# Centring of the second channel norm: 128 tokens in one matmul, or 64 tokens on each half of the array

## The chip, the core and the metric

One core of a Trainium2 chip. The metric is the device time of one execution in microseconds (us). The engines work in parallel, each through its own list of instructions, and meet by semaphores: TensorE (PE, with its weight loads PEld), VectorE (DVE), ScalarE (ACT), GpSimd (POOL) and SyncE (SP), which issues DMAs. TensorE reads SBUF and writes PSUM, whose 8 banks of 512 floats in each of 128 partitions are the tensor PS here.

## What is computed

An image x of 8 x 32 x 64 x 64 (batch, channels, height, width) in float32 goes through two blocks. Cut to what matters:

```python
x = x + L0_conv(ln_c(x))      # spectral convolution, by DFT matmuls
t = to_tokens(x)              # a token: the 32 channels of a pixel
t = t + L0_ffn(ln_t(t))       # soft routing, 16 experts
x = from_tokens(t, x)
x = x + L1_conv(ln_c(x))      # four sweeps of a 9-tap convolution, row by row
t = to_tokens(x)
t = t + L1_ffn(ln_t(t))
```

ln_c takes the mean over the 32 channels of a pixel, and divides by the root of the variance. The change is in the second ln_c, ahead of the four sweeps.

## The kernel before

**Layout.** The 128 partitions of an image hold 4 batch entries x 32 channels; a row of 8192 floats has two batch halves of 4096 pixels. RA, RB, RC, RD (RC and RD are the halves of RCD) and RE are the large SBUF regions. Work goes in 8 groups of 1024 columns, each with one slot of two PSUM banks, ln_slot(g) = banks 2(g % 4) and 2(g % 4) + 1.

**A channel norm, group by group** (norm_tokens on each engine). centre_group(ln, g) on TensorE: eight matmuls; the weights (the stationary operand) are 128 columns of the image, that is 128 pixels, and the moving operand is the 128 x 128 matrix centre (in dft_sb), which subtracts the mean over each 32 channels. The result has a pixel per partition and 128 columns (batch, channel). A float32 matmul leaves two records on PE and two on PEld. Then ACT squares the slot into RE (line 780), DVE sums over 32 channels (line 912), ACT takes the root (line 762), and DVE the reciprocal (line 919) and the product (line 928, "norm g"). follower(g) on TensorE waits for that. In the second norm it is turn_rows: eight transposes (line 725) of the normed group back into the slot, which ACT copies to RD with drain_follower (line 769).

**The second norm.** Pixels of a group are taken 4 columns apart (src = RC[:, first + n % Q:first + BANK:Q], Q = 4), since the sweeps want them sorted by column modulo 4. It starts inside the first expert layer: 16 scatter matmuls of 512 columns (line 714) give the layer's output, DVE adds each to RC (line 940), and behind the sixth and the tenth (FED) TensorE does centring groups 0 and 1.

**What sets the order.** Each engine's order is written out by hand. TensorE: scatter matmuls with groups 0 and 1 between; follower 0; groups 2 and 3; then follower g and group g + 3 in turn; followers 5 to 7. Group g from 4 on needs follower g - 4 copied out of its slot; groups 2 and later need all 16 adds. DVE: six adds, sum 0, four adds, norm 0, sum 1, six adds, norm 1, sums 2 and 3, norm 2, then sum g + 1 ahead of norm g. ACT: Square g behind the copy of follower g - 3, then root g - 1. The convolution (TensorE line 745, DVE line 1141) starts when all copies are done. It and the pooling (line 664) use the halves of the array: two matmuls with 64 weight columns each, whose outputs go to partitions 0 to 63 and 64 to 127. So does the spectral mixing (line 533).

Of the kernel before, what the change touches and what calls it, by code (L numbers as in the profile page):

```python
# [21 lines left out]
MO = P // 2  # L22
# [18 lines left out]
def build_kernel(nc, x_in, dft, wspec, conv_w, conv_b, gate_w, gate_b, w1, w2, b2, own, out):  # L41
# [5 lines left out]
    with ExitStack() as ctx:  # L47
        def sb(name, shape, dt=F32):
            return ctx.enter_context(nc.sbuf_tensor(name, shape, dt))
# [5 lines left out]
        RA, RB, RCD = sb("RA", [P, NF]), sb("RB", [P, NF]), sb("RCD", [P, 2 * NF])  # L55
# [6 lines left out]
        centre, ident, fwd_w, fwd_h, inv_h, inv_w = (dft_sb[:, i, :] for i in range(6))  # L62
# [64 lines left out]
        def blk(region, n):  # L127

            return region[:, n * P:(n + 1) * P]

        def banks(b0, nb):
            return PS[:, b0:b0 + nb, :].rearrange("p k c -> p (k c)")
# [103 lines left out]
        def ln_slot(g):  # L236

            return banks(2 * (g % 4), 2)
# [195 lines left out]
        def _(pe):  # L434
# [9 lines left out]
            def centre_group(ln, g):  # L444

                if ln == 0:
                    pe.wait_ge(s_x[g], 16)
                else:
                    pe.wait_ge(s_ad, 2 * g + 2 if g < 2 else 16)
                if g >= 4:  # L450
                    pe.wait_ge(s_fd, 8 * ln + g - 3)
                for n in range(8):
                    if ln == 0:
                        src = blk(RA, 8 * g + n)
                    else:
                        first = 1024 * g + BANK * (n // Q)
                        src = RC[:, first + n % Q:first + BANK:Q]
                    m = pe.matmul(blk(ln_slot(g), n), src, centre, start=True, stop=True)  # L458
                m.then_inc(s_cen, 1)

            def norm_tokens(ln, follow):

                def follower(g):
                    pe.wait_ge(s_nrm, 8 * ln + g + 1)
                    follow(g).then_inc(s_ff, 1)

                if ln == 1:
                    follower(0)
                for g in range(2 * ln, 4):
                    centre_group(ln, g)  # L470
                for g in range(ln, 8):
                    follower(g)
                    if 1 <= g < 5:
                        centre_group(ln, g + 3)
# [20 lines left out]
            for l in range(2):  # L495
                m = pe.matmul(PS[:, 6 + l, 0:BL * NE], centre, gate_sb[:, l, :], start=True, stop=True)
# [50 lines left out]
            for c in range(NCH):  # L547
# [5 lines left out]
                for w, full, read in ((1, s_t1, s_tmp), (0, s_t0, s_comb)):  # L553
                    if c >= 2:
                        pe.wait_ge(read, c - 1)
                    for x in range(X8):
                        m = pe.transpose(blk(banks(4 * (c % 2) + 2 * w, 2), x), Z[:, c, x, w], ident)  # L557
# [60 lines left out]
            def experts(l):  # L618
# [87 lines left out]
                for k in range(16):  # L706
                    if k >= 4:
                        pe.wait_ge(s_ad, 16 * l + k - 3)
                    if l == 0:
                        bh, ch = divmod(k, 8)  # L710
                    else:
                        ch, bh = divmod(k, 2)
                    rhs = CW[l][:, ch * BANK:(ch + 1) * BANK]
                    pe.matmul(PS[:, 4 + k % 4, :], espread[:, BL * bh:BL * bh + BL, :].rearrange("p b o -> p (b o)"), rhs,  # L714
                              start=True, stop=True).then_inc(s_sc, 1)
                    if l == 0 and k in FED:
                        centre_group(1, FED.index(k))
# [15 lines left out]
            for bank in range(2 * len(CHAINS)):  # L733
                m = pe.matmul(PS[:, bank, 0:P], warm[:, :], warm[:, :], start=True, stop=True)
# [485 lines left out]
```

## Time and profile before

| | |
|---|---|
| time, median of 3 | 612.09 us (611.95, 612.09, 614.93) |
| profiled execution, span | 614.5 us (of the three times only 614.93 is as long as that) |
| TensorE busy, weight loads | 565.0 us (92%), 511.2 us (83%) |
| DVE, ACT, POOL busy | 351.7, 319.6, 115.1 us |
| mean granted TensorE clock | 0.967 of full speed |
| second channel norm | from about 240 to 292 us of the span |

The span runs from the first to the last instruction. "Busy" of TensorE counts a record from its start to its modelled end, so that overlapping records of a pipeline fill the time. The chain of waits is followed back from the last instruction, at each step to what released it. A granted clock of 1.00 is 2.4 GHz, of 0.50 is 1.2 GHz.

### The profile page before, as it was taken

The page shows a single profiled execution, that of the slowest core. Times are in us where ns is not written, and L with a number is a line of the kernel's source. Part 1 is how long each engine was busy: PE and PEld are TensorE (multiplying, and loading weights), DVE is VectorE, ACT ScalarE, POOL GpSimd, SP SyncE. Part 2 cuts the span into 40 slices and gives each one's busy share as a digit, 9 for nine tenths or more (in the row PEclk, how much of TensorE's full clock was granted, in tenths as well). Part 3 has the DMA queues.
Part 4 walks back from the last instruction along what each step waited for, and adds up shares of the span by engine and source line. Part 5 has one row for each costly group of instructions (what it writes and reads, how often), then busy time and mean ns, then how long its engine had stood idle before and what let it go on. Part 6 is the DMA issues. An engine that isn't in the chain of part 4 may idle for free.

```text
span 614.5 us, 22679 instructions
## 1 busy us (share of the span) xinstructions
PE 565.0 (92%) x9860; PEld 511.2 (83%) x9860; DVE 351.7 (57%) x813; ACT 319.6 (52%) x842; POOL 115.1 (19%) x240
## 2 busy tenths in 40 slices
PE   8978878999999899997999999969999999984997
PEld 8978877999998897797899988868888888984973
DVE  2657989557435943755455455435555455568736
ACT  4766979452348610254444444424445777568610
POOL 4000000000016000000233333383332034371000
PEclk9999999899999798998899999989999999998989
DMA  9830764060000000000000003340000144500007
GB/s 352 330 137 2 276 234 181 2 246 29 1 2 1 2 3 19 0 1 0 3 5 3 5 3 89 90 105 4 4 3 5 25 76 83 102 1 1 2 3 273
DMA packets 50250, 41.53 MB, mean 68 GB/s; under 512 B 44998, under 2 KB 45126, under 8 KB 48934
## 3 DMA queue, kind: packets, MB, share of 16 engines
q1 hardware_dynamic: 49304, 38.51, 19.4%
q8 instruction: 79, 1.29, 0.9%
q0 software_dynamic: 704, 1.18, 0.9%
q10 hardware_dynamic: 144, 0.39, 0.2%
q14 instruction: 19, 0.16, 0.1%
HBM read 27.49 MB, written 4.19 MB: 52 GB/s over the span
## 4 chain that ended last, share of the span: by engine, by line
PE 76%; DVE 12%; ACT 5%; POOL 4%; issue 2%; DMA 1%; SPq 0%; POOLq 0%; ACTq 0%
PE PS L745 38%; PE PS L458 6%; PE PS L714 5%; DVE RB L986 4%; PE PS L479 3%; PE PS L533 3%; PE PS L664 3%; PE PS L608 2%; PE PS L557 2%; PE PS L564 2%; POOL RCD L400 2%; POOL RE L397 2%; PE PS L578 2%; PE PS L638 2%; DVE sums L1025 1%
## 5 line engine op out<-in xcount | busy, mean ns | idle before, releaser
L745 PE MATMUL PS<-RE,conv_sb 128*64 128x64 f32 x6048 | 230.9, 229 | 5.1 <-DVE RE L1129 4.7
L745 PEld LDWEIGHTS PS<-RE,conv_sb 128*64 128x64 f32 x6048 | 205.3, 139 | 30.8 <-DVE RE L1129 5.4
L879 ACT COPY PS<-convb_sb 128x64 f32<-128x64 f32 x504 | 108.2, 215 | 113.3 <-DVE RE L1141 89.2
L1141 DVE SCALAR_TENSOR_TENSOR RE<-PS,RCD 128x64 f32<-128x64 f32 x252 | 56.6, 225 | 58.2 <-PE PS L745 50.1
L409 POOL COPY RCD<-RE 128x128 f32<-128x128 f32 x126 | 37.0, 294 | 166.6 <-DVE RE L1141 166.4
L1141 DVE SCALAR_TENSOR_TENSOR RE<-PS,RE 128x64 f32<-128x64 f32 x126 | 32.5, 258 | 27.9 <-PE PS L745 19.9
L808 ACT COPY RB<-PS 32x256 f32<-32x256 f32 x64 | 42.4, 662 | 7.5 <-PE PS L517 6.8
L986 DVE COPY RB<-PS 32x256 f32<-32x256 f32 x64 | 42.2, 659 | 6.0 <-PE PS L517 5.2
L1141 DVE SCALAR_TENSOR_TENSOR RE<-PS,RB 128x64 f32<-128x64 f32 x126 | 28.3, 225 | 28.1 <-PE PS L745 19.9
L479 PE MATMUL PS<-warm 128*128 128x128 bf16 x468 | 37.8, 253 | 7.1 <-ACT RCD L848 4.5
L533 PE MATMUL PS<-RE,RB 128*64 128x64 f32 x1024 | 33.6, 228 | 9.8 <-issue 4.1
L533 PEld LDWEIGHTS PS<-RE,RB 128*64 128x64 f32 x1024 | 32.5, 143 | 11.2 <-issue 6.2
L479 PEld LDWEIGHTS PS<-warm 128*128 128x128 bf16 x468 | 35.0, 116 | 8.1 <-ACT RCD L848 4.7
L912 DVE TENSOR_REDUCE sums<-RE 128x32 f32<-128x1024 f32 x16 | 19.4, 1218 | 34.1 <-ACT RE L780 34.1
L397 POOL TENSOR_TENSOR RE<-RA 128x1024 f32<-128x1024 f32 x3 | 5.7, 1892 | 173.7 <-ACT RA L841 173.7
L780 ACT ACTIVATE RE<-PS 128x1024 f32<-128x1024 f32 x16 | 16.2, 1021 | 33.1 <-PE PS L458 33.0
L1025 DVE TENSOR_REDUCE sums<-RE 128x32 f32<-128x1024 f32 x16 | 19.2, 1201 | 24.2 <-POOL RE L397 18.7
L458 PEld LDWEIGHTS PS<-dft_sb,RCD 128*128 128x128 f32 x128 | 30.5, 328 | 0.9 <-issue 0.5
L458 PE MATMUL PS<-dft_sb,RCD 128*128 128x128 f32 x128 | 30.8, 396 | 0.0
L769 ACT COPY RCD<-PS 128x256 f32<-128x256 f32 (+1 forms) x40 | 24.7, 692 | 11.0 <-PE PS L725 5.8
L827 ACT COPY RB<-PS 128x512 f32<-128x512 f32 (+1 forms) x24 | 16.2, 736 | 26.2 <-PE PS L564 26.2
L714 PE MATMUL PS<-RCD,espread 128*128 128x512 f32 x64 | 29.7, 618 | 0.0
(120 smaller groups left out, 780.1 us busy)
## 6 DMA issues: line engine op xcount, KB each, us to landing
RE<-wspec SPq DMA_DIRECT2D x8, 2048.0 KB, 8.8
RA<-x_in SPq DMA_DIRECT2D x8, 512.0 KB, 7.5
RCD<-x_in SPq DMA_DIRECT2D x1, 4096.0 KB, 13.3
out<-RA SPq DMA_DIRECT2D x8, 512.0 KB, 2.7
RCD<-RB SPq DMA_DIRECT2D x58, 64.0 KB, 2.5
RE<-RCD SPq DMA_DIRECT2D x32, 80.0 KB, 2.6
conv_sb<-conv_w SPq DMA_DIRECT2D x1, 768.0 KB, 20.0
w_sb<-w SPq DMA_DIRECT2D x2, 264.0 KB
```

What stands on the lines that cost most here:

```text
L409: pool.tensor_copy(o, i).then_inc(s_arc, 1)
L458: m = pe.matmul(blk(ln_slot(g), n), src, centre, start=True, stop=True)
L479: pe.matmul(PS[:, bank, 0:P], warm[:, :], warm[:, :], start=True, stop=True)
L533: m = pe.matmul(o[:, x % 2, y], XB[:, c % 2, x, 2 * y + a].rearrange("p r q b -> p (r q b)"), WR[:, c % 3, a, x, y, :], start=True, stop=True)
L714: pe.matmul(PS[:, 4 + k % 4, :], espread[:, BL * bh:BL * bh + BL, :].rearrange("p b o -> p (b o)"), rhs, start=True, stop=True).then_inc(s ...
L745: m = pe.matmul(conv_bank(s, u, c)[o:o + OC], conv_sb[:, s, d, o:o + OC], prev, start=False, stop=(d == 2), skip_group_check=True)
L769: m = act.copy(o, i)
L808: m = act.copy(o, i)
L879: act.copy(banks_of, convb_sb[:, s:s + 1].unsqueeze(2).to_broadcast([P, c1 - c0, n])).then_inc(s_seed, 1)
L986: m = dve.tensor_copy(o, i)
L1025: dve.tensor_reduce(sums[:, 32 * g:32 * g + 32], square[:, g % 2, 0:1024].rearrange("p (a c) -> p a c", c=C), AX_X, ALU.add).then_inc(s_su ...
L1141: dve.scalar_tensor_tensor(out=state[:, state_slot(s, u), b0:b1, 1:1 + HO], in0=conv_bank(s, u, c), scalar=0.0, in1=row_at(SRC[s], s, q, u ...
```

## The change

In the second norm each centring matmul becomes two. The one takes the first 64 of the 128 pixels as weights and writes partitions 0 to 63 of the same 128 PSUM columns, the other the last 64 and partitions 64 to 127; the moving operand is the whole matrix centre both times. The first norm keeps its matmul, now written in its own branch.

```diff
                 for n in range(8):
                     if ln == 0:
-                        src = blk(RA, 8 * g + n)
+                        m = pe.matmul(blk(ln_slot(g), n), blk(RA, 8 * g + n), centre, start=True, stop=True)
                     else:
                         first = 1024 * g + BANK * (n // Q)
                         src = RC[:, first + n % Q:first + BANK:Q]
-                    m = pe.matmul(blk(ln_slot(g), n), src, centre, start=True, stop=True)
+                        for a in range(2):
+                            toks = slice(MO * a, MO * (a + 1))
+                            m = pe.matmul(blk(ln_slot(g), n)[toks], src[:, toks], centre, start=True, stop=True)
                 m.then_inc(s_cen, 1)
```

MO is 64, Q is 4, BANK is 512. All lines behind it move down by two: 458 is 460 in the second norm, 714 is 716, 725 is 727.

TensorE, from the scatter matmuls to centring groups 2 and 3, before (form of the output; an x for equal instructions in a row):

```order
L714 MATMUL PS<-RCD,espread 128x512 x6
L458 MATMUL PS<-dft_sb,RCD 128x128 x8
L714 MATMUL PS<-RCD,espread 128x512 x4
L458 MATMUL PS<-dft_sb,RCD 128x128 x8
L714 MATMUL PS<-RCD,espread 128x512 x6
L725 MATMUL PS<-dft_sb,RA 128x128 x8
L458 MATMUL PS<-dft_sb,RCD 128x128 x16
L725 MATMUL PS<-dft_sb,RA 128x128 x8
```

and after:

```order
L716 MATMUL PS<-RCD,espread 128x512 x6
L460 MATMUL PS<-dft_sb,RCD 64x128 x16
L716 MATMUL PS<-RCD,espread 128x512 x4
L460 MATMUL PS<-dft_sb,RCD 64x128 x16
L716 MATMUL PS<-RCD,espread 128x512 x6
L727 MATMUL PS<-dft_sb,RA 128x128 x8
L460 MATMUL PS<-dft_sb,RCD 64x128 x32
L727 MATMUL PS<-dft_sb,RA 128x128 x8
```

The places are the same; at each centring group stand 16 matmuls with 64 output partitions where there were 8 with 128.

TensorE in the steady part, follower 2 and centring group 5, with the waits (ln_normed is DVE's norm, follower_drained ACT's copy), before:

```order
L725 MATMUL PS<-dft_sb,RA 128x128 [waits ln_normed]
L725 MATMUL PS<-dft_sb,RA 128x128 x7
L458 MATMUL PS<-dft_sb,RCD 128x128 [waits follower_drained,scatter_added]
L458 MATMUL PS<-dft_sb,RCD 128x128 x7
```

and after:

```order
L727 MATMUL PS<-dft_sb,RA 128x128 [waits ln_normed]
L727 MATMUL PS<-dft_sb,RA 128x128 x7
L460 MATMUL PS<-dft_sb,RCD 64x128 [waits follower_drained,scatter_added]
L460 MATMUL PS<-dft_sb,RCD 64x128 x15
```

The waits are the same, and each stands on the first matmul of the group, as before.

DVE in the steady part after the change, sum 4, norm 3, sum 5 and norm 4 (squared comes from ACT, std_ready from ACT's root):

```order
L914 TENSOR_REDUCE sums<-RE 128x32 [waits squared]
L921 RECIPROCAL rstd<-std 128x32 [waits std_ready]
L930 TENSOR_TENSOR RA<-PS,rstd 128x4x4x32 [waits rstd_ready]
L930 TENSOR_TENSOR RA<-PS,rstd 128x4x4x32
L914 TENSOR_REDUCE sums<-RE 128x32 [waits squared]
L921 RECIPROCAL rstd<-std 128x32 [waits std_ready]
L930 TENSOR_TENSOR RA<-PS,rstd 128x4x4x32 [waits rstd_ready]
L930 TENSOR_TENSOR RA<-PS,rstd 128x4x4x32
```

Here nothing moved but the line numbers (each 2 more than before): the sum of a group stands ahead of the norm of the group before it.

## Rows read from the trace of the kernel before

**Rows 1.** The page, parts 1 and 4: busy shares and the chain by engine and line.

```profile
span 614.5 us, 22679 instructions
...
PE 565.0 (92%) x9860; PEld 511.2 (83%) x9860; DVE 351.7 (57%) x813; ACT 319.6 (52%) x842; POOL 115.1 (19%) x240
...
PE 76%; DVE 12%; ACT 5%; POOL 4%; issue 2%; DMA 1%; SPq 0%; POOLq 0%; ACTq 0%
PE PS L745 38%; PE PS L458 6%; PE PS L714 5%; DVE RB L986 4%; PE PS L479 3%; PE PS L533 3%; PE PS L664 3%; PE PS L608 2%; PE PS L557 2%; PE PS L564 2%; POOL RCD L400 2%; POOL RE L397 2%; PE PS L578 2%; PE PS L638 2%; DVE sums L1025 1%
```

**Rows 2.** Chain of waits in order of time (start us, us, what, records).

```profile
31.16 1.80 PE PS L458 x16
...
240.82 3.61 PE PS L458 x16
...
247.86 3.61 PE PS L458 x16
251.47 5.15 PE PS L714 x12
256.62 0.87 PE PS L725 x8
257.50 7.66 PE PS L458 x32
265.16 0.87 PE PS L725 x8
266.03 3.73 PE PS L458 x16
269.76 0.87 PE PS L725 x8
```

**Rows 3.** Weight loads by form (xcount, busy us, mean ns, idle before, releaser).

```profile
L458 PEld LDWEIGHTS PS<-dft_sb,RCD 128*128 128x128 f32 x128 | 30.5, 328 | 0.9 <-issue 0.5 <-DVE RCD L940 0.2
...
L458 PEld LDWEIGHTS PS<-dft_sb,RA 128*128 128x128 f32 x128 | 15.3, 199 | 0.0
```

**Rows 4.** Loads of lines 458, 654, 664, 564 (ns min/median/max).

```profile
L458 PEld LDWEIGHTS PS<-dft_sb,RA x128: 192/192/333, 5.8 to 32.6; 128*128 128x128 f32 x128
...
L458 PEld LDWEIGHTS PS<-dft_sb,RCD x128: 307/330/330, 240.2 to 283.0; 128*128 128x128 f32 x128
...
L654 PEld LDWEIGHTS PS<-dft_sb,rsum x2: 84/84/84, 212.2 to 573.7; 128*1 128x1 f32 x2
...
L664 PEld LDWEIGHTS PS<-RE,RA x256: 133/138/138, 216.1 to 225.8; 128*64 128x64 f32 x128
...
L564 PEld LDWEIGHTS PS<-dft_sb,RA x64: 185/192/209, 127.9 to 142.7; 128*128 128x128 f32 x64
```

**Rows 5.** Timeline of one steady group (start us, us, engine, line; idle before in brackets).

```profile
269.60 1.04 PE L725 MATMUL PS<-dft_sb,RA 128*128 128x128 f32 x8
269.80 1.02 ACT L780 ACTIVATE RE<-PS 128x1024 f32<-128x1024 f32 x1 [2.29 <-PE PS L458]
...
270.47 3.89 PE L458 MATMUL PS<-dft_sb,RCD 128*128 128x128 f32 x16
270.72 0.31 ACT L762 ACTIVATE std<-sums,eps_sb 128x32 f32<-128x32 f32 x1
270.86 1.22 DVE L912 TENSOR_REDUCE sums<-RE 128x32 f32<-128x1024 f32 x1 [1.80 <-ACT RE L780]
270.93 1.18 ACT L769 COPY RCD<-PS 128x256 f32<-128x256 f32 x4
271.99 0.34 DVE L919 RECIPROCAL rstd<-std 128x32 f32<-128x32 f32 x1
272.37 1.29 DVE L928 TENSOR_TENSOR RA<-PS,rstd 128x512 f32<-128x512 f32 x2
273.97 1.03 PEld L725 LDWEIGHTS PS<-dft_sb,RA 128*128 128x128 f32 x8
274.20 1.04 PE L725 MATMUL PS<-dft_sb,RA 128*128 128x128 f32 x8
```

**Rows 6.** Windows of the first norm, the steady part, the wait and the last followers.

```profile
core 0: us, PE busy (x) PEld busy (x) DVE busy (x) ACT busy (x) POOL busy (x), PEclk, DMA share, GB/s
5.00:35.00 30.00, 27.49 (x234) 26.73 (x232) 18.22 (x20) 21.19 (x22) 2.66 (x1) 1.00 0.79 315
257.00:285.00 28.00, 27.44 (x141) 27.04 (x139) 14.55 (x22) 12.71 (x31) 0.00 (x0) 1.00 0.00 1
285.00:286.00 1.00, 0.00 (x0) 0.00 (x0) 1.00 (x2) 0.08 (x1) 0.00 (x0) 1.00 0.00 0
288.00:289.00 1.00, 1.00 (x6) 1.00 (x6) 1.00 (x2) 0.00 (x0) 0.00 (x0) 0.50 0.00 0
```

**Rows 7.** Chain of waits: transposes and matmuls on halves of the array.

```profile
65.51 3.95 PE PS L533 x128
...
141.30 1.78 PE PS L564 x16
...
216.21 1.99 PE PS L664 x64
218.20 1.02 PE PS L674 x8
219.23 1.99 PE PS L664 x64
```

**Rows 8.** Timeline: DVE's sum and six adds behind centring group 1.

```profile
252.56 1.22 DVE L912 TENSOR_REDUCE sums<-RE 128x32 f32<-128x1024 f32 x1 [1.85 <-ACT RE L780]
...
253.70 3.67 DVE L940 TENSOR_TENSOR RCD<-PS,RCD 128x512 f32<-128x512 f32 x6
```

**Rows 9.** Timeline: TensorE in centring groups 2 and 3.

```profile
257.43 7.73 PE L458 MATMUL PS<-dft_sb,RCD 128*128 128x128 f32 x32
...
265.00 1.04 PE L725 MATMUL PS<-dft_sb,RA 128*128 128x128 f32 x8
```

**Rows 10.** Timeline: the last two followers.

```profile
287.52 3.38 PE L725 MATMUL PS<-dft_sb,RA 128*128 128x128 f32 x16 [3.08 <-DVE RA L928]
```

## Prediction

> **What bounds the kernel now.** I began with the chain of waits, since it says whose time is on the path: TensorE has 76% of the span there, and line 458, the centring, 6% [rows 1]. The busy shares alone would not have told this, as TensorE is at 92% everywhere. In order of time the chain shows two different line 458s [rows 2]. In the first channel norm a group of eight centrings (16 records, two per float32 matmul) takes 1.80 us; in the second the same 16 records take 3.61, 3.61, 7.66 for two groups, and then some 3.73 four times, with 0.87 of turning transposes (line 725) between: 4.60 us a group. The second norm's eight centring groups are thus some 30 us of path.
>
> Why twice as long? The groups by form [rows 3] show the weight loads: 199 ns mean where the 128 tokens lie side by side (RA), 328 ns where they lie 4 floats apart (RCD, src = RC[:, first + n % Q : first + BANK : Q]). A load of 1 column takes 84 ns, of 64 columns 138, of 128 columns 192 (the median of line 458 on RA [rows 4]): a fixed 84 and then 0.84 ns a column. A strided load has 307 at its shortest and 330 at the median [rows 4]: less 84 that is 223 to 246, or 1.74 to 1.92 ns a column. The pace, 3.61/16 = 226 ns a record, is this streaming time. The moving side is no bound: a transpose, with 128 moving columns too, keeps 0.87/8 = 109 ns a record. So here TensorE waits for its own weight loads, which a shorter load can help.
>
> In the steady part TensorE is never idle, while ACT waits 2.29 us for each centring group and DVE 1.80 us for each Square [rows 5]. The granted clock there is 1.00 (2.4 GHz) [rows 6].
>
> **The change, part by part.** Each of the 64 matmuls of the second norm becomes two: 64 tokens as weights, the same 128 columns of centre moving, output rows 0 to 63 or 64 to 127 of the same bank columns. No wait, no semaphore count and no order between groups changes; the first norm's branch keeps its matmul. Per group there are 32 records for 16, so 128 loads and 128 matmul records are added in all.
>
> *What a pair of records costs.* No row of before shows a strided load on half the columns. Nearest are the pooling matmuls of line 664: 64-column contiguous loads on the same two halves of the array, 32 columns moving. 64 records take 1.99 us [rows 7], 62 ns a pair. Each load alone streams 138 - 84 = 54 ns, so two in turn would need 108: the halves load side by side, with 7 or 8 ns on top. Line 533, with 64 moving columns, has 128 records in 3.95 us [rows 7], again 62 ns a pair, so the moving side of a half (about 54 ns) hides behind the next load as well. I carry this over: a strided 64-column load streams 64 x 1.74 = 111 to 64 x 1.92 = 123 ns, the moving side of a half needs at most the 109 above, and a pair takes 111 + 8 = 119 to 131 ns. I take 122, near the lower end, since the pace of 226 per 128 columns (113 for 64) is measured on the engine and the 330 includes time waiting for the array. A group is then 16 x 122 = 1.95 us, where it was 3.61 to 3.79. Bounds from rows: not under 16 x 109 = 1.75, not over 16 x (226 + 8) = 3.75 if the loads of the halves take turns, and 7.1 in the case of the third rival.
>
> *Going between whole array and halves.* Eight transposes take 1.02 us between two stretches of line 664 [rows 7] and 0.87 elsewhere: 0.15 us for there and back. Three of these fall on the path outside the loop below (groups 0 and 1, and groups 2 and 3 together): 0.45 us. Inside the loop I put them into the follower, 1.02 for 0.87.
>
> *Groups 0 and 1*, between the scatter matmuls of line 714: TensorE sets the pace, so 2 x (3.61 - 1.95) = 3.32 us come off, if DVE keeps up. From the end of centring 1, TensorE asks for the last scatter add after six scatter matmuls of 0.86 (5.15 for six [rows 2]) and follower 0: 6.2 us. By then ACT and DVE have to do 0.20 and 1.06 until the sum starts, the sum 1.22 and six adds 3.67 [rows 5, 8]: 6.15 us. The cover just holds; where it doesn't, tenths of a us are lost.
>
> *Groups 2 and 3* stand back to back: 7.57 us from issue to issue (257.43 to 265.00 [rows 9]) become 3.90, so 3.67 off.
>
> *Groups 4 to 7.* Here the whole 2 x (3.73 - 1.95) per two groups cannot be had, since another bound comes up. DVE's queue has the sum of group g+1 ahead of the norm of group g, and follower g must run before centring g+3. So norm g releases follower g (0.05), 1.02, centring g+3 1.95, 0.20 until Square starts, 1.06 until the sum starts, and 2.80 from there to the end of norm g+2 (269.60, 269.80, 270.86 and 272.37 + 1.29 [rows 5]). That is 7.08 us for two groups, where TensorE's own work is 2 x (1.95 + 1.02) = 5.94. Now two groups take 9.20 (265.00 to 269.60 and on to 274.20 [rows 5, 9]). Norm 2 to norm 6 is two such rounds: 2 x (9.20 - 7.08) = 4.24 off. What is late next is therefore not TensorE but the round over four engines; TensorE will stand idle about 1.1 us in 7.
>
> *Sum.* 3.32 + 3.67 + 4.24 - 0.45 = **10.8 us**. Behind norm 6 nothing changes: two followers at half clock (16 records in 3.38 us [rows 10], granted 0.50 [rows 6]) after a wait of 3.08 us, and the convolution, which starts as soon as the copies end. I expect the same wait and the same half clock, only earlier. For any group time x the saving is 2(3.61 - x) + (7.57 - 2x) + 2(9.20 - max(5.13 + x, 2(x + 1.02))) - 0.45; the rivals use it.
>
> The profiled execution spans 614.5 us, more than two of the three times, so of those it can only be the one of 614.93, with 0.43 around the span. Its span would be 603.7. It is 2.84 above the median, which one trace cannot place; the stage here ran at full clock, so I take the whole saving from the median: 612.09 - 10.8 = **601.3 us**. With 1.75 it would be 12.0, with 2.25 it would be 9.0.
>
> *A rule on strides.* The loads take twice as long at a distance of 16 bytes [rows 3]. The Trainium skill's page "SBUF — State Buffer" (section "Specifications (TRN2)") says that the memory is read in lines of 16 bytes, that full speed needs at least two reads in a line, and that each step to a new line is charged. The trace agrees with that for one load. The page does not say whether two loads at once would share the charge; if the memory itself is the limit, it is the second rival.
>
> **The rivals.**
> *Part of the gain.* The halves' loads disturb each other, halfway between 1.95 and 3.75: at x = 2.8 the saving is 1.62 + 1.97 + 2.54 - 0.45 = 5.7, 606.4 us. For it: strided groups slow from 226 to 237 ns a record (7.57/32) where ACT and DVE are busy, so they do share something. Chance 0.13.
>
> *Loads in turns.* Both halves read one line per token, so that the memory hands out 128 tokens per 226 ns as before, and the doubled records bring nothing: x = 3.75, the saving is -0.28 + 0.07 - 0.68 - 0.45 = -1.3, 613.4 us, no change. Against it: the transposes of line 564 read tokens 8 floats apart, 185 to 209 ns a load, and still keep 1.78/16 = 111 ns a record [rows 4, 7], so lines can come twice as fast as line 458 takes them. Chance 0.11.
>
> *Slower: loads not hidden.* A 64-column load waits until the other half's matmul is through, so load and matmul of each record follow one another, 113 + 109 = 222 ns: x = 32 x 0.222 = 7.1, -6.98 - 6.63 - 14.08 - 0.45 = 28.1 slower, 640.2 us. It decides from x about 4.0 on: there the loss passes 3 us. Against it stand both stretches of 62 ns a pair [rows 7]. Chance 0.06.
> The Trainium skill's page "TensorE: Matmul & The Clock Gate" (Part 3, "The mechanism") states this rule: a load overlaps running matmuls only if its row group differs, and both halves here use all rows. Lines 533 and 664 use all rows too and overlap, so the trace speaks against it.
>
> *The clock falls.* With TensorE idle 1.1 us in 7, the granted clock could drop from group 4 on. With every record twice as long, as in the last followers [rows 10], TensorE's work in a round would be 2 x (2 x 1.75 + 2 x 1.02) = 11.0, the saving 3.32 + 3.67 - 3.6 - 0.45 = 2.9, 609.2 us. Against it: the first norm has TensorE idle 2.5 of 30 us at a clock of 1.00 [rows 6], and the fall in the second norm came only behind the 3 us wait. Chance 0.02.
>
> **How the numbers follow.** The forecast, 9 to 12 us off, has 0.68. Range 599.0 to 609.5: below, 12.0 off and 1 us for the difference between runs (the three of before span 3.0); above, the case of part of the gain with the same room, and the fallen clock. It leaves out turns, not hidden loads and a little of the forecast's edge, 2 in 10. Half a percent, 3.1 us, is about what a measurement of this kernel can tell from no change: faster by more 0.79 (forecast and part, less their edges), within 0.15 (turns, clock, edges), slower 0.06.
>
> **What the profile after will show.** Line 460 with 64-column loads near 195 ns (84 + 111) and 1.95 us a group of 32 records in the chain: if 3.7, loads take turns; if 7, they are not hidden. Norm to norm 3.55 us in the steady part with TensorE idle before followers 4 and 6; if TensorE is never idle, x is over 3. Centring group 2 starts near 254.4, where it was 257.43. The convolution's step is unchanged, and starts near 282. The prediction is wrong if the pair costs more than 140 ns, or if the clock is 0.50 for longer than in the two last followers.

## The result, and the profile after

The changed kernel takes 603.9 us, median of 600.15, 603.02, 604.78 and 607.85; the kernel before, with a fourth run, 612.02. The ratio is 0.9836, with a 95% interval from 0.980 to 0.9872. Two more sets of runs of the same two kernels gave 602.37 beside 615.33, ratio 0.9799 (0.9751 to 0.9848), and 605.65 beside 613.88, ratio 0.987 (0.9831 to 0.991). In each of the three later sets one slow run of the kernel before (621.63, 620.91 and 622.13) is left out. The ratios are those on record and not the quotients of these medians, 0.9867, 0.9789 and 0.9866, which lie inside the intervals. So the kernel is faster by 1.3 to 2.0%; the single runs of the changed kernel lie between 599.8 and 609.6.

The page of the profiled execution (603.02 us), span and part 1, to be set beside [rows 1]:

```profile
span 601.2 us, 22935 instructions
...
PE 552.6 (92%) x9988; PEld 499.7 (83%) x9988; DVE 350.6 (58%) x813; ACT 318.9 (53%) x842; POOL 115.1 (19%) x240
```

There are 128 more records on PE and on PEld each, as counted ahead. TensorE's busy time is 12.4 us less, the other engines have theirs within 1.1 us. The chain of waits in the second norm, in order of time (start us, us, what, records); it answers to [rows 2]:

```profile
231.47 6.13 PE PS L716 x12
237.60 2.12 PE PS L460 x31
239.73 3.63 PE PS L716 x8
243.36 2.12 PE PS L460 x32
245.47 5.35 PE PS L716 x12
250.82 0.87 PE PS L727 x8
251.70 4.06 PE PS L460 x64
...
259.70 1.09 PE PS L727 x8
260.79 2.15 PE PS L460 x32
...
262.96 1.04 ACT RE L782
...
264.02 1.22 DVE sums L914
265.24 0.27 DVE rstd L921
...
265.54 1.30 DVE RA L930 x2
...
266.88 1.09 PE PS L727 x8
267.97 2.14 PE PS L460 x32
...
274.05 3.62 PE PS L727 x16
...
278.95 0.41 PE PS L736 x4
```

A group of centrings takes 2.12 to 2.15 us where it took 3.61 to 3.83, two back to back 4.06 where they took 7.66. And the chain has changed its kind. Before, it went from line 458 to line 725 and back, TensorE alone. Now it goes follower, centring, Square (line 782), sum (line 914), reciprocal (921), norm (930) and to the next follower but one: the round over four engines. The matmuls and loads of line 460 by duration (ns min/median/max), beside [rows 4]:

```profile
L460 PEld LDWEIGHTS PS<-dft_sb,RCD x256: 192/209/218, 237.5 to 269.7; 128*64 128x64 f32 x128
L460 PE MATMUL PS<-dft_sb,RCD x256: 281/283/388, 237.5 to 269.8; 128*64 128x128 f32 x128
```

The load has gone from 307/330/330 to 192/209/218. Inside a group the loads of one half start 120 ns apart, and those of the other half 7 ns behind them; before, the loads started 233 ns apart. Pieces of TensorE's timeline, behind the scatter matmuls and in the steady part, beside [rows 5, 9]:

```profile
243.29 2.00 PEld L460 LDWEIGHTS PS<-dft_sb,RCD 128*64 128x64 f32 x32 [0.76 <-DVE RCD L942]
243.29 2.19 PE L460 MATMUL PS<-dft_sb,RCD 128*64 128x128 f32 x32
...
256.69 2.00 PEld L460 LDWEIGHTS PS<-dft_sb,RCD 128*64 128x64 f32 x32 [0.17 <-issue]
...
259.70 1.09 PE L727 MATMUL PS<-dft_sb,RA 128*128 128x128 f32 x8 [0.83 <-DVE RA L930]
...
274.05 3.60 PE L727 MATMUL PS<-dft_sb,RA 128*128 128x128 f32 x16 [2.94 <-DVE RA L930]
```

The loads of the same group in the kernel before:

```profile
247.27 4.00 PEld L458 LDWEIGHTS PS<-dft_sb,RCD 128*128 128x128 f32 x16 [0.24 <-issue]
```

The first row says that the loads stood idle for 0.76 us behind those of the scatter matmuls; between loads of line 716 it is 0.24, and so it was ahead of the first load of line 458. The row names DVE's add, but this group needs the first four adds only, and the last scatter matmul ahead of it had itself waited for six. What differs is this: in the kernel before, the first centring load starts together with the last record of the scatter matmuls, in the changed one 0.52 us behind that start. The idle 0.83 ahead of the follower at 259.70 is new: TensorE has time over. Before the follower at 274.05 it waits 2.94, where it waited 3.08 [rows 10].

From the start of the first centring group to the four warm matmuls ahead of the convolution it was 292.20 - 240.82 = 51.38 us before and is 278.95 - 237.60 = 41.35 after: **10.03 us off**. From there to the end it is 322.3 in both (614.5 - 292.20, 601.2 - 278.95). The remaining 3.2 us between the two spans lie ahead of the change.

### The profile page after: what moved, and what is told of

It reads as the page before. It is cut to its first block, busy times and chain, and to the rows that moved or that the text cites. A ratio compares the mean times of both kernels' runs of the same rounds, so it can differ in the third digit from the quotient of the medians.

```text
span 601.2 us, 22935 instructions
## 1 busy us (share of the span) xinstructions
PE 552.6 (92%) x9988; PEld 499.7 (83%) x9988; DVE 350.6 (58%) x813; ACT 318.9 (53%) x842; POOL 115.1 (19%) x240
## 4 chain that ended last, share of the span: by engine, by line
PE 71%; DVE 16%; ACT 6%; POOL 4%; issue 2%; DMA 1%; SPq 0%; POOLq 0%; DVEq 0%; ACTq 0%
PE PS L747 38%; PE PS L716 5%; DVE RB L988 5%; PE PS L666 3%; PE PS L610 2%; PE PS L559 2%; PE PS L566 2%; PE PS L460 2%; PE PS L535 2%; POOL RCD L400 2%; POOL RE L397 2%; PE PS L580 2%; PE PS L640 2%; DVE RCD L1064 1%; DVE sums L1027 1%
## 5 line engine op out<-in xcount | busy, mean ns | idle before, releaser
L747 PEld LDWEIGHTS PS<-RE,conv_sb 128*64 128x64 f32 x6048 | 209.0, 138 | 25.7 <-DVE RE L1131 4.6
L481 PE MATMUL PS<-warm 128*128 128x128 bf16 x468 | 35.5, 244 | 6.3 <-ACT RCD L850 3.6
L535 PE MATMUL PS<-RE,RB 128*64 128x64 f32 x1024 | 31.8, 223 | 8.1 <-DVE RCD L997 3.9
L481 PEld LDWEIGHTS PS<-warm 128*128 128x128 bf16 x468 | 32.7, 111 | 7.3 <-ACT RCD L850 4.0
L535 PEld LDWEIGHTS PS<-RE,RB 128*64 128x64 f32 x1024 | 30.8, 138 | 9.3 <-issue 4.7
L409 POOL COPY RB<-RE 128x128 f32<-128x128 f32 x63 | 18.5, 294 | 40.0 <-DVE RE L1143 40.0
L716 PEld LDWEIGHTS PS<-RCD,espread 128*128 128x128 f32 x64 | 12.9, 208 | 15.0 <-issue 14.5
```

The costliest lines, as they stand in the source:

```text
L409: pool.tensor_copy(o, i).then_inc(s_arc, 1)
L535: m = pe.matmul(o[:, x % 2, y], XB[:, c % 2, x, 2 * y + a].rearrange("p r q b -> p (r q b)"), WR[:, c % 3, a, x, y, :], start=True, stop=True)
L747: m = pe.matmul(conv_bank(s, u, c)[o:o + OC], conv_sb[:, s, d, o:o + OC], prev, start=False, stop=(d == 2), skip_group_check=True)
```

## Experiments

Two lengths are used below. A *group* is the chain's time for eight centrings. The *norm stretch* runs from the first centring group of the second norm to the warm matmuls: 51.38 us before, 41.35 after. (The expectations speak of a stretch that begins with the first scatter matmul, six matmuls earlier: 56.95 and 47.48. Those six took anything from 5.6 to 7.2 us from run to run with the granted clock, so the readings here begin behind them.) Of six of the kernels there is one execution each: 615.53 us (one half after the other), 605.20 and 605.72 (without the distance, whole array and halves), 604.68 (halves in the first norm), 604.76 (quarters) and 617.14 (the kernel before in the new order). From these the lengths of stages are read, not gains in total time.

### One half after the other

Theory: the gain comes from the loads of the two halves running side by side. Rival: a short load is cheaper by itself.

```diff
-                for n in range(8):
+                for a, n in ((a, n) for a in range(1 + ln) for n in range(8)):
```

(and the inner loop over a goes.) 

> The same 16 matmuls of a centring group, but all eight on the lower half of the array first and then all eight on the upper half. Theory (the gain is that the strided weight loads of the two halves run side by side): records that follow one another on one half load in turn, 113 to 125 ns each, so a group of 32 records takes 3.6 to 4.0 us, where the changed kernel shows 2.0 to 2.1 and the kernel before 3.6 to 3.8; the stretch from the first scatter matmul of layer 0 to the warm matmuls ahead of the convolution takes 56 to 59 us (before 56.95, after 47.48). Rival (a shorter load is cheaper by itself, whichever half comes next): a group stays at 2.0 to 2.1 us and the stretch at 47 to 48.

The chain in the steady part, and the loads:

```profile
264.28 1.03 PE PS L726 x8
265.31 3.66 PE PS L459 x32
268.97 1.03 PE PS L726 x8
```

```profile
L459 PEld LDWEIGHTS PS<-dft_sb,RCD x256: 193/209/218, 240.3 to 282.6; 128*64 128x64 f32 x128
```

A group takes 3.66 us, 114 ns a record, and TensorE is the bound again. The norm stretch is 51.47 us (240.36 to 291.83), that of before to 0.1 us; from the first scatter matmul it is 57.64, inside the forecast. The loads themselves last as long as in the changed kernel, 209 ns at the median. So the rival falls: the same loads, in another order, bring nothing. Within one half the records start 120 ns apart (the mean of 114 is lower because the loads overlap for a few records where one half follows the other). In the changed kernel a pair of them, one on each half, starts every 120 ns too: side by side, the two loads do not slow each other. The run took 615.53 us, beside 615.33 for the kernel before.

### Without the distance of 4 floats

```diff
-                        first = 1024 * g + BANK * (n // Q)
-                        src = RC[:, first + n % Q:first + BANK:Q]
+                        src = blk(RC, 8 * g + n)
```

once with the whole array and once with halves. Both kernels leave out the order that the sweeps want, so only their times are of use. 

> Whole-array matmuls as before, but the weights are 128 neighbouring columns of the image instead of columns 4 apart, so the pixels come out in another order than the sweeps want. Theory (the distance of 4 floats is what the loads cost): a group takes 1.8 us as in the first norm, loads have 192 ns, and the stretch takes 44 to 46 us. Rival (the second norm is slow because ACT and DVE use SBUF at the same time): loads stay over 250 ns and a group over 2.5 us.

> Halves of 64 as in the changed kernel, but with neighbouring columns as weights (again in another order than the sweeps want). Theory (in the changed kernel a pair's 125 to 130 ns are the strided load): with loads of 138 ns the moving side is the bound, 109 to 117 ns a pair, 1.75 to 1.87 us a group. Rival (the 125 to 130 ns are the hand-over between the halves): a group stays at 2.0 to 2.1 us.

Whole array, the chain and the loads:

```profile
262.59 1.09 PE PS L721 x8
263.69 1.80 PE PS L454 x16
```

```profile
L454 PEld LDWEIGHTS PS<-dft_sb,RCD x128: 186/192/192, 241.2 to 271.9; 128*128 128x128 f32 x128
```

Halves, the chain and the loads:

```profile
260.95 1.09 PE PS L726 x8
262.04 1.92 PE PS L459 x32
```

```profile
L459 PEld LDWEIGHTS PS<-dft_sb,RCD x256: 132/137/137, 239.6 to 270.5; 128*64 128x64 f32 x128
```

With neighbouring columns the whole array takes 1.80 us a group, as in the first norm, while ACT and DVE do the same work beside it: the distance was the cost, not the neighbours on SBUF. Halves take 1.90 to 1.92 a group, above the forecast of 1.75 to 1.87. Inside the group a pair starts every 109 ns, the pace of the moving side (0.87/8) and the lower edge of the forecast for a pair, so the hand-over between halves costs nothing there. The other 0.18 us (1.92 - 16 x 0.109) lie at the ends of the group, between whole array and halves; the second pair starts 160 ns behind the first. The changed kernel's 120 ns a pair is 11 ns off this floor. The norm stretch is 39.23 us with the whole array and 40.00 with halves. So the distance costs the changed kernel 1.35 us beside halves without it, and 2.12 beside the whole array, where it cost 12.15 before (51.38 - 39.23). From the first scatter matmul the whole array takes 46.43 us, more than the 44 to 46 forecast; the six scatter matmuls ahead took 7.20 there.

### Halves in the first norm too

```diff
                     if ln == 0:
-                        m = pe.matmul(blk(ln_slot(g), n), blk(RA, 8 * g + n), centre, start=True, stop=True)
+                        src = blk(RA, 8 * g + n)
...
+                    for a in range(2):
+                        toks = slice(MO * a, MO * (a + 1))
+                        m = pe.matmul(blk(ln_slot(g), n)[toks], src[:, toks], centre, start=True, stop=True)
```

> Halves in the first norm too, whose weight columns lie side by side. Theory (halves pay only where the load is longer than the 109 ns of the moving side): the first norm's group goes from 1.80 us to 1.85 to 1.95 plus the change between whole array and halves, so nothing is gained there, and its stretch is 0 to 1.5 us longer. Rival (halves pay everywhere): a group there takes under 1.6 us.

The chain in the first norm (line 460 are the centrings, line 490 the followers):

```profile
17.13 2.05 PE PS L490 x16
19.18 1.90 PE PS L460 x32
21.08 1.98 PE PS L490 x16
...
36.70 2.07 PE PS L490 x16
```

1.90 for 1.80 [rows 2], and the followers between halves take 1.98 where they take 1.79 in the changed kernel. From the first to the last follower it is 36.70 - 17.13 = 19.57 us, in the changed kernel 36.24 - 17.22 = 19.02. Halves pay where the load is longer than the moving side, and cost half a us where it isn't.

### Quarters

```diff
-                        for a in range(2):
-                            toks = slice(MO * a, MO * (a + 1))
+                        for a in range(4):
+                            toks = slice(C * a, C * (a + 1))
```

> Four quarters of 32 tokens instead of two halves. Theory (loads of different column tiles run side by side until the moving side, some 109 ns for 128 columns, is the bound): a strided 32-column load streams 56 to 62 ns, so the four records of a pass take 110 to 120 ns and a group of 64 records 1.75 to 1.95 us, where halves take 2.0 to 2.1. Rival (the side-by-side loads share something, as 114 ns alone on a half and 126 to 130 for a pair suggest): over 2.2 us a group.

```profile
L460 PEld LDWEIGHTS PS<-dft_sb,RCD x512: 134/136/159, 241.9 to 272.9; 128*32 128x32 f32 x171
```

```profile
264.37 1.96 PE PS L460 x64
```

The load is down to 136 ns at the median, the group to 1.91 to 1.96 us, as with neighbouring columns: the moving side binds, and four records start every 109 ns. Two steady groups take 270.27 - 263.27 = 7.00 us where they took 7.18, though TensorE is not the bound: one centring lies on the round over the engines, and the round is shorter by what this centring is. The norm stretch is 39.27 us, 2.08 less than in the changed kernel. Of that, 0.92 lie behind norm 6, where the last two followers kept a granted clock of 1.00:

```profile
277.25 1.09 PE L727 MATMUL PS<-dft_sb,RA 128*128 128x128 f32 x8 [2.96 <-DVE RA L930]
278.84 1.09 PE L727 MATMUL PS<-dft_sb,RA 128*128 128x128 f32 x8 [0.49 <-DVE RA L930]
```

The wait ahead of them is that of the changed kernel. Why the clock did not fall here is open; the 1.16 us that are left are the shorter groups.

### The round behind group 3

Theory: from group 4 on the round of four engines is the bound. Then another order on DVE and ACT should help the changed kernel, and not the one before.

```diff
+                if ln == 1:
+                    for g in range(2, 8):
+                        norm(g)
+                        if g < 7:
+                            total(g + 1)
+                    return
```

and on ACT, root(g - 1) ahead of Square g for g from 3 on. In the changed kernel: 

> The changed kernel, with DVE's norm g put ahead of the sum of group g+1, and ACT's root of group g-1 ahead of Square g, in the second norm alone. Theory (behind group 3 the round norm g, follower g, centring g+3, Square, sum, norm g+2 is the bound, 7.18 us for two groups, not TensorE): the round becomes one of three groups, 0.05 + 1.09 + 2.14 + 0.20 + 1.06 + 1.2 + 0.4 + 1.7 = 7.8 us, under TensorE's own 3 x 3.15; a steady group takes 3.1 to 3.2 us where it took 3.59, and the stretch from the scatter to the warm matmuls 44 to 46 us where it took 47.3 to 47.5: 2 to 3 us off. Rival (TensorE or DVE's own work is already the bound): the stretch stays within 0.5 us of 47.4.

In the kernel before: 

> The same reordering of DVE and ACT in the kernel before, whole-array centrings of 3.61 to 3.83 us. Theory (there TensorE is the bound in the steady part): a steady group stays at 4.60 us, and only the tail behind the last centring can get shorter, by the sum of group 7 that no longer stands ahead of norm 6: the stretch takes 55 to 57 us (before 56.95). Rival (the order of DVE was a bound there too): a steady group under 4.4 us and the stretch under 55.

The chain of the first in the steady part:

```profile
262.85 1.29 DVE RA L932 x2
264.14 1.14 DVE sums L916
...
265.30 0.33 ACT std L764
...
265.66 0.36 DVE rstd L923
...
266.04 1.29 DVE RA L932 x2
```

A steady group takes 3.19 us (266.04 - 262.85) where it took 3.59, and the norm stretch 39.88 us, 1.5 less. With the scatter it is 46.08, just above the 44 to 46 forecast, and 1.3 to 1.4 off where 2 to 3 were expected. TensorE has no waits left in the steady part, a follower and a centring every 3.14 us, as expected. But what ends last is a round that the expectation did not name. It lies between DVE and ACT alone: norm 1.29, sum 1.14, root 0.33, reciprocal 0.36 and the gaps. That it is as long as TensorE's own pace is luck. In the kernel before, the steady group stays at 4.60, and the norm stretch is 49.85: 1.5 off at the tail only (from the first scatter matmul 57.03, with 55 to 57 forecast). So the round is the bound only where centring is short. The time, 604.17 us beside 614.79, ratio 0.9831 (0.9787 to 0.9875), can't be told from the changed kernel's, which was not run in this set.

### The waits behind the last centring

Three kernels in one set: the changed one again, the changed one with dummy matmuls in TensorE's waits, and one with the new order and dummies fitted to it (28, 34 and 20).

```diff
                 for g in range(ln, 8):
                     follower(g)
+                    if ln == 1 and g >= 5:
+                        pe.wait_ge(s_fd, 13)
+                        keep_warm(0, (50, 0, 20)[g - 5])
```

> The changed kernel beside the next two, on the same chip. Theory: 599 to 605 us, with 47.2 to 47.6 us from the first scatter matmul of layer 0 to the warm matmuls ahead of the convolution, of which some 1.7 are the last two followers at half clock.

> The changed kernel with dummy matmuls on a free PSUM bank in TensorE's waits behind the last centring: 50 behind follower 5 and 20 behind follower 7. Theory (the wait of 2.9 us ahead of follower 6 is what lets the granted clock fall, and 1.7 us of the gain and some 1.2 us of the first convolution steps are lost to it): followers 6 and 7 take 1.9 to 2.1 us together where they take 3.6, the stretch is 45.6 to 46.2 us, the first steps of the convolution run at full clock, and the median is 2 to 3 us under the changed kernel's. Rival (the fall comes whatever TensorE does there, or the dummies only delay follower 6): the stretch stays at 47 us or more.

> DVE's norm ahead of the next sum (as in the run of that name) and dummy matmuls behind followers 5, 6 and 7 (28, 34, 20). Theory: the stretch loses the 1.3 us of the new order and the half clock of follower 7 too: 44.5 to 45.5 us, and the median is 3 to 4 us under the changed kernel's. Rival (what is won in the norm is lost in the convolution or elsewhere): the stretch is at 45, and the median within 1.5 us of the changed kernel's.

TensorE's timeline behind the last centring, with the dummies (line 484):

```profile
271.77 1.09 PE L730 MATMUL PS<-dft_sb,RA 128*128 128x128 f32 x8
272.70 2.96 PE L484 MATMUL PS<-warm 128*128 128x128 bf16 x50
275.81 1.09 PE L730 MATMUL PS<-dft_sb,RA 128*128 128x128 f32 x8
277.48 1.06 PE L730 MATMUL PS<-dft_sb,RA 128*128 128x128 f32 x8 [0.58 <-DVE RA L933]
```

The granted clock stays at 1.00, and each of the two last followers takes 1.1 us where both took 3.6. The norm stretch is 40.46 us beside 41.28, only 0.8 less: the second follower now waits for norm 7. By the stretch from the first scatter matmul, in which the forecasts are worded, it is 47.66 beside 47.56, so the forecast of 45.6 to 46.2 failed; the six scatter matmuls took 7.20 us there for 6.28. With the new order the norm stretch is 38.98, 2.3 less (from the scatter 45.33, as forecast). That the dummies keep the clock up is not shown beyond doubt. It fell about the last followers in ten of the eleven traces without dummies, and in neither of the two with them; but with quarters it stayed at 1.00 behind the same wait. Nor does the convolution gain, as was expected: its first steps ran at 1.00 in all three traces, and from the warm matmuls to the end it is 323.7 us with the dummies, 322.1 in the changed kernel and 321.2 with the new order. The medians are 605.65, 601.41 and 601.05 us; the ratios to before 0.987 (0.9831 to 0.991), 0.9818 (0.9783 to 0.9853) and 0.9786 (0.976 to 0.9812). The last is the fastest median here, and its interval stands clear of the changed kernel's of the same set. What the medians differ by beyond 2.3 us is not from the norm stretch, and in the second set the changed kernel itself came to 0.9799; the 2.3 us are shown by the trace, not by the medians. Three median forecasts were missed: 605.65 for 599 to 605, and 4.2 and 4.6 us under the changed kernel for 2 to 3 and 3 to 4.

### Where the spread comes from

> The changed kernel once more, for its time and its spread. Theory: the stretch from the scatter to the convolution gives 9.5 to 10.5 us in every run, and the rest of the spread comes from stages that the change does not touch: a median between 600 and 604 us beside 612. Rival (the gain is partly given back in the convolution): the stretch gives 10 us, and the median lies at 604 or above.

The median, 602.37, is as forecast. The norm stretch is 41.35, 41.32 and 41.28 us in three profiled executions of the changed kernel, whose spans are 601.2, 599.9 and 604.8. The stage of the change does not spread; the spans do. The chain of the second:

```profile
42.99 7.01 PE PS L439 x64
```

```profile
107.27 3.95 PE PS L535 x128
```

and of the third:

```profile
42.31 8.68 PE PS L439 x64
```

```profile
110.29 5.50 PE PS L535 x128
```

Two stages that the change does not touch, the transposes ahead of the spectral stage and a group of its mixing, make 3.2 of the 4.9 us. The records there are the same ones, only longer, as at the lower granted clock (0.83 from 40 to 50 us of the third run, 1.00 in the second). The convolution gives nothing back: from the warm matmuls to the end it is 322.2 and 322.1 us.

## Why the prediction was right, point by point

**The bound and the pair.** Right: the strided weight load was what TensorE waited for (1.80 us without the distance), and two halves load side by side (3.66 us if they can't). For a pair 122 ns was taken, from a range of 119 to 131; inside a group it starts every 120, which is the pace of one half alone. Nothing is left of the 8 ns on top. Yet a group takes 2.12 to 2.15 us and not 1.95: the 0.2 us beyond 16 x 0.120 lie at its ends, between whole array and halves (the second pair's matmuls start 222 ns behind the first's, the next follower 220 behind the last pair).

**Groups 0 and 1.** Mis-sized: 3.02 with the changes between halves and whole array, 2.59 measured (2 x (3.61 - 2.12), less 0.19 and 0.20 that the scatter matmuls behind them take longer). The term that was too small is the 0.15 for the change to halves and back; measured, it is some 0.37 (2.12 - 1.95, and 0.19 or 0.20 behind). The 0.15 was read on transposes with 128 columns. Behind a scatter matmul with 512 columns the first load of a half is idle for 0.76 us where the whole array's is for 0.24, since it no longer goes on under the running matmul. Halves without the distance and quarters show the same 0.76, the whole array without the distance 0.24: it belongs to the halves, not to the distance.

**Groups 2 and 3.** 3.67 - 0.15 forecast, 7.66 - 4.06 = 3.60 measured: between transposes the 0.15 was about right.

**Groups 4 to 7.** The step that mattered: not 2 x 1.78 for two groups but what the round leaves. Forecast 7.08 us for two groups, measured 266.88 - 259.70 = 7.18, with TensorE idle 0.83 and 0.82 us ahead of followers 2 and 4. From follower 1 to follower 6 it was 287.52 - 265.16 = 22.36 and is 274.05 - 255.76 = 18.29: 4.07, forecast 4.24. The order of DVE and ACT, and the kernel before with the same order, show that the round is the bound.

**The tail.** The same wait and the same half clock as forecast (2.94 us, then 3.62 for 3.40). The sum is 2.59 + 3.60 + 4.07 - 0.22 = 10.04, forecast 10.8. The medians of the three sets differ by 8.1, 13.0 and 8.2: each lies outside the 9 to 12 that the stage in the traces confirms, and that 603.9 came within 2.6 us of the 601.3 is in part luck.

**What failed.** The step on the profiled execution's own time. It took 614.5 us of span for the run of 614.93. In all later runs 1.75 to 1.89 us lie around the span, so this execution took some 616.3, as an estimate, and was none of the three. The saving was rightly set against the median. And the difference between runs was put too small: 1 us of room, where the changed kernel's own runs differ by 10. In the rival of the falling clock the round adds up to 11.08 us and not 11.0, which changes nothing else.

**The rivals.** Part of the gain, loads in turns and loads not hidden fall with the group times. The 226 and 237 ns that spoke for the first are means over whole groups; inside every group of the kernel before, groups 0 and 1 too, the loads start 233 ns apart. Halves without the distance start a pair every 109 ns, all of it the moving side, which leaves no room for loads of 54 in sequence. So the rule of the Trainium skill's page "TensorE: Matmul & The Clock Gate" (Part 3, "The mechanism"), that a load overlaps matmuls only of another row group, does not hold for halves that use all rows. Two loads of columns 4 floats apart run side by side, 120 ns for both as for one alone. On the lines of 16 bytes of the Trainium skill's page "SBUF — State Buffer" (section "Specifications (TRN2)") this decides, for this case, what the page leaves open. The clock did not fall before the last wait. It was at 0.50 again from 281 to 284 us, in the first steps of the convolution; the kernel before has the same from 294 to 297, so the sign of being wrong that asks for 0.50 in the last two followers only was badly chosen.

## What to carry to other kernels

If weight loads are slow because of a stride in the free dimension, splitting the stationary operand into column tiles lets several slow loads run at once: here two halves came to 120 ns a pair, and four quarters to the 109 of the moving side. The matmuls of the tiles must alternate, and where loads are already hidden it costs a little, as does each change between whole array and tiles. When a stage is bound by one engine alone, walk the round of waits through the others before counting the whole saving: here 9.20 us of TensorE hid a round of 8.9 (an estimate, 5.13 + 3.73 by the prediction's terms), so that of 2.9 us saved on TensorE in two groups only 2.0 arrived. A shorter centring still shortens the round, as the quarters show, because it is one of its steps. Read a small change from the length of its own stage in the trace, if the whole kernel spreads by more than its effect.

## What was not expected of the hardware

Two strided loads on the halves of the array start every 120 ns as a pair, as often as one of them alone. A load for a half that follows a 512-column matmul on the whole array does not start under it (0.76 us of idle loads, 0.24 for whole after whole). With dummy matmuls in a wait of 3 us the granted clock stayed at 1.00, and each follower took 1.1 us; yet only 0.8 of the 1.4 us reached the end of the stretch, and the run with quarters shows the same clock without dummies.
